# A transformer layer on one core: the order of stages drawn again from a planner with other costs

## The reference

```python
x = x + 0.5 * ffn(layernorm(x))
x = x + attention(layernorm(x))
x = x + 0.5 * ffn(layernorm(x))
```

## Time and profile before

| | us |
|---|---|
| median of 3 executions | 1149.53 |
| lowest and highest of them | 1144.08, 1149.84 |
| profiled execution, its own time | 1146.77 |
| its span, first to last instruction | 1145.5 |
| PE busy | 1014.8 |
| DVE busy | 728.5 |
| ACT busy | 642.0 |
| POOL busy | 486.2 |
| mean granted TensorE clock | 0.963 |

### The profile page before, as it was taken

The page is one execution under the profiler, slowest core; times in us unless marked ns, Lnnn a source line. Parts: engine busy times, 40 slices in busy tenths (PEclk is TensorE's granted clock), DMA queues, the critical chain, the costliest instruction groups (busy, mean ns, idle before and its releaser), DMA issues. The chain is left out here.

```text
span 1145.5 us, 11321 instructions
## 1 busy us (share of the span) xinstructions
PE 1014.8 (89%) x3424; PEld 559.0 (49%) x3424; DVE 728.5 (64%) x1210; ACT 642.0 (56%) x1100; POOL 486.2 (42%) x449
## 2 busy tenths in 40 slices
PE   5989999779899898899999799978997999999992
PEld 3456544446345554344554445444554544446671
DVE  2310119879799988979998999899999721200000
ACT  4334334775674776655687666339778733224441
POOL 3444540556414334335334324714654412245642
PEclk9989999899999899999999899989999999999997
DMA  9966563793834776825587953347885735226666
GB/s 317 328 184 132 97 166 82 192 275 62 207 101 92 172 205 164 223 66 141 126 218 163 228 156 84 94 124 177 177 212 134 167 46 96 70 92 112 129 100 111
DMA packets 69201, 172.53 MB, mean 151 GB/s; under 512 B 12579, under 2 KB 12579, under 8 KB 67015
## 3 DMA queue, kind: packets, MB, share of 16 engines
q0 software_dynamic: 32576, 72.44, 34.8%
q1 hardware_dynamic: 35270, 89.74, 25.0%
q10 hardware_dynamic: 1296, 9.63, 2.4%
HBM read 112.86 MB, written 68.33 MB: 158 GB/s over the span
## 5 line engine op out<-in xcount | busy, mean ns | idle before, releaser
L932 PE MATMUL yps<-w_all,hidden_sb 128*128 x424 | 212.5, 626 | 15.7 <-ACT hidden_sb L1098 15.5
L916 PE MATMUL hps<-w_all,hidden_sb 128*128 x848 | 206.9, 389 | 11.0 <-ACT hidden_sb L1081 10.7
L1720 POOL DMA_INDIRECT xs<-x_normal,rows_i x106 | 121.8, 1149 | 198.9 <-PE xps L907 141.6
L916 PEld LDWEIGHTS hps<-w_all,hidden_sb 128*128 128x128 f32 x848 | 159.7, 195 | 49.4 <-issue 31.1
L1744 POOL DMA_INDIRECT x_rows<-ys,rows_i x56 | 105.2, 1878 | 147.6 <-ACT ys L1111 137.9
L1520 DVE TENSOR_TENSOR_SCAN run<-pwx,trig 128x512 f32<-128x512 f32 x128 | 149.4, 1209 | 20.8 <-ACT trig L1186 20.4
L1111 ACT ACTIVATE ys<-yps,slots 128x512 f32<-128x512 f32 x106 | 72.6, 686 | 110.8 <-PE yps L932 80.4
L932 PEld LDWEIGHTS yps<-w_all,hidden_sb 128*128 128x128 f32 x424 | 80.8, 200 | 87.9 <-issue 85.5
L874 PE MATMUL yps<-sw_sb,hidden_sb 128*128 128x512 f32 x256 | 120.1, 613 | 0.0
L862 PE MATMUL hps<-xnT,sw_sb 128*128 128x512 f32 x256 | 117.8, 612 | 2.1 <-issue 2.1
L1706 POOL DMA_INDIRECT slots<-told,dest_i x64 | 78.1, 1220 | 51.0 <-DVE cmp_a L1389 32.2
(11 more groups left out here) (201 smaller groups left out, 1541.8 us busy)
## 6 DMA issues: line engine op xcount, KB each, us to landing
qx<-q_cols SPq DMA_DIRECT2D x64, 512.0 KB
w_all<-in_w_experts SPq DMA_DIRECT2D x8, 1024.0 KB
x_normal<-xin SPq DMA_DIRECT2D x32, 256.0 KB
xin<-x_rows SPq DMA_DIRECT2D x32, 256.0 KB, 7.1
turns_sb<-in_w_out ACTq DMA_DIRECT2D x3, 1536.0 KB, 7.9
xin<-in_x SPq DMA_DIRECT2D x16, 256.0 KB, 6.0
sum_rows<-ys SPq DMA_DIRECT2D x16, 256.0 KB
xin<-sum_rows POOLq DMA_DIRECT2D x16, 256.0 KB, 5.9
```

The source lines that it names most:

```text
L916: t = PE.matmul(hps[:, bank, 0:H], xT[:, j % 2, c, :], w_all[:, bass.ds(expert[j] + c * H, H)], start=c == 0, stop=c == KC - 1)
L932: t = PE.matmul(yps[:, bank, :], hb[:, j % 2, ec, :], w_all[:, bass.ds(expert[j] + (KC * H + ec * D), D)], start=ec == 0, stop=ec == EC - 1)
L1720: GE.indirect_dma_start(xs[:, j % NX, :], None, xn_rows[PAIR_OF[g]], bass.IndirectOffsetOnAxis(rows_i[:, g % 2, j:j + 1], 0)).then_inc(*xs ...
```

## The change

Costs, crossings and offsets of the planner are replaced. Stages, their instructions, waits and buffers are the same; only the lists of ORDERS differ, and with them the counts at which semaphores are awaited. A cost was the length of a stage; now it is the time from one stage of the engine to the next, and HOP, charged for every step from a stage to a follower, is 0.2 instead of 0.1. The core of the diff (the rest of the costs are lowered in the same manner, by 0.08 to 1.1 us):

```diff
-                piece("PE", s, 3.6, *kept_rows, *start[:1], *blocks_end, bank=[("hps", ("ACT", s))])
-                piece("ACT", s, 0.7, ("PE", s), *([("PE", ("acc", q - 1, TB - 1))] if q else []), table="gelu")
+                piece("PE", s, 3.45, *kept_rows, *start[:1], *blocks_end, bank=[("hps", ("ACT", s))])
+                piece("ACT", s, 0.58, ("PE", s), *([("PE", ("acc", q - 1, TB - 1))] if q else []), table="gelu")
...
-                piece("PE", s, 0.6 if j % AT_ONCE else 1.3, ("POOL", ("bring", g, j), 3.8),
+                piece("PE", s, 0.45 if j % AT_ONCE else 0.95, ("POOL", ("bring", g, j), 3.8),
...
-                piece("PE", s, 1.86, ("ACT", ("x", g, j)),
+                piece("PE", s, 1.74, ("ACT", ("x", g, j)),
...
-                piece("PE", s, 0.4, ("ACT", ("one", g, j)))
-                piece("ACT", s, 0.8, ("PE", s), *([("PE", ("two", g, j - 2))] if j >= 2 else []), table="gelu")
+                piece("PE", s, 0.23, ("ACT", ("one", g, j)))
+                piece("ACT", s, 0.52, ("PE", s), *([("PE", ("two", g, j - 2))] if j >= 2 else []), table="gelu")
...
-                piece("PE", s, 1.86, ("ACT", ("mid", g, j)), bank=[("yps", ("ACT", s))])
-                piece("ACT", s, 0.7, ("PE", s),
+                piece("PE", s, 1.73, ("ACT", ("mid", g, j)), bank=[("yps", ("ACT", s))])
+                piece("ACT", s, 0.59, ("PE", s),
...
-            piece("ACT", ("c_turn", b, n), 2.0, ("DVE", ("c_turn", b, n)), table="sin")
+            piece("ACT", ("c_turn", b, n), 1.81, ("DVE", ("c_turn", b, n)), table="sin")
...
-                    piece("PE", s, 1.9, ("SP", ("c_out", b, half), 2.4), ("SP", ("w_bd",), 12.0), *rows_before_it,
+                    piece("PE", s, 1.73, ("SP", ("c_out", b, half), 3.8), ("SP", ("w_bd",), 12.0), *rows_before_it,
...
-        PARTS = {"job": {2: 652, 3: -380, 4: -82, 6: -504},
-                 "blocks": {1: -389, 3: 798},
+        PARTS = {"job": {2: -357, 4: -260, 6: -1496},
+                 "blocks": {0: 1007, 1: 101, 4: 10},
                  "head": {},
-                 "tail": {0: -319, 1: 1414, 2: -298, 3: 283},
-                 "steps": {2: 407}}
+                 "tail": {1: 27},
+                 "steps": {1: -1517}}
-        KINDS = {("ACT", "mid"): -175,
-                 ("ACT", "norm"): 880,
-                 ("ACT", "o_rows"): 556,
-                 ("ACT", "one"): -59,
-                 ("ACT", "x"): -132,
...
-                 ("PE", "gT"): -2768,
-                 ("PE", "hidden"): -415,
...
+        KINDS = {("ACT", "a_q"): -279,
+                 ("ACT", "a_spread"): -58,
+                 ("ACT", "mid"): -725,
+                 ("ACT", "one"): -188,
+                 ("ACT", "two"): -1518,
+                 ("ACT", "x"): -67,
...
+                 ("DVE", "c_times"): -1129,
+                 ("DVE", "c_turn"): -88,
...
+                 ("PE", "hidden"): -1850,
+                 ("PE", "mid"): 3087,
...
         URGENT = {
-            ("ACT", "c_turn"): {0: -804, 1: 297},
-            ("ACT", "two"): {2: -35, 4: -95},
-            ("DVE", "c_turn"): {0: -25, 1: 1196, 2: -92, 3: -968},
...
+            ("ACT", "c_turn"): {2: -89},
+            ("ACT", "mid"): {1: -1518},
+            ("DVE", "c_turn"): {3: 312},
...
-        HOP = 0.1
+        HOP = 0.2
```

More of the change, by code:

```diff
@@ L335, in plan_job @@
-            piece("ACT", ("chunks", q), 0.6, ("PE", ("chunks", q)), *([("PE", ("logits", q - 1))] if q else []))
-            piece("PE", ("logits", q), 0.9, ("ACT", ("chunks", q)), *start[2:], bank=[("xps", ("DVE", ("rank", q)))])
-            piece("DVE", ("rank", q), 1.7, ("PE", ("logits", q)), *start[2:], *([("DVE", ("gates", q - 1))] if q else []),
+            piece("PE", ("chunks", q), 1.0, *kept_rows, *start[:1], bank=[("xps", ("ACT", ("chunks", q)))])
+            piece("ACT", ("chunks", q), 0.48, ("PE", ("chunks", q)), *([("PE", ("logits", q - 1))] if q else []))
@@ L338, in plan_job @@
+            piece("PE", ("logits", q), 0.8, ("ACT", ("chunks", q)), *start[2:], bank=[("xps", ("DVE", ("rank", q)))])
+            piece("DVE", ("rank", q), 1.5, ("PE", ("logits", q)), *start[2:], *([("DVE", ("gates", q - 1))] if q else []),
                   *([("DVE", ("place", g - 1))] if g and not second else []))
-            piece("ACT", ("gates", q), 0.3, ("DVE", ("rank", q)), *([("DVE", ("gates", q - 1))] if q else []), table="exp")
-            piece("DVE", ("gates", q), 1.7, ("ACT", ("gates", q)), *([("PE", ("gT", q - 1))] if q else []),
+            piece("ACT", ("gates", q), 0.15, ("DVE", ("rank", q)), *([("DVE", ("gates", q - 1))] if q else []), table="exp")
@@ L341, in plan_job @@
+            piece("DVE", ("gates", q), 1.5, ("ACT", ("gates", q)), *([("PE", ("gT", q - 1))] if q else []),
                   *([("POOL", ("scatter", g - 2, GTS[g - 2] // 2 - 1), 2.0)] if g > 1 else []))
-            piece("PE", ("gT", q), 0.7, ("DVE", ("gates", q)), bank=[("xps", ("DVE", ("gT", q)))])
-            piece("DVE", ("gT", q), 0.7, ("PE", ("gT", q)), *([("PE", ("acc", q - 1, TB - 1))] if q else []))
+            piece("PE", ("gT", q), 0.45, ("DVE", ("gates", q)), bank=[("xps", ("DVE", ("gT", q)))])
@@ L344, in plan_job @@
+            piece("DVE", ("gT", q), 0.6, ("PE", ("gT", q)), *([("PE", ("acc", q - 1, TB - 1))] if q else []))
             blocks_end = [("PE", ("two", g - 1, NBS[g - 1] - 1))] if g and not second else []
@@ L402, in plan_blocks @@
                     last = [("SP", ("w_rows", JOBS[q][1]), 12.0) for q in GROUPS[g]] if JOBS[z][0] == 1 else []
[L403 removed]
+                piece("POOL", ("add", g, j), 1.65, ("ACT", s), *last)
             if JOBS[z][0] == 2:
@@ L431, in plan_head @@
                 free += [("DVE", ("a_den", b - 1))] if i == HALVES and b else []
-                piece("PE", s, 3.7, *kept_rows, weights, *free, *before, bank=[("misc", ("DVE", s))])
+                piece("PE", s, 3.45, *kept_rows, weights, *free, *before, bank=[("misc", ("DVE", s))])
                 piece("DVE", s, 3.0, ("PE", s))
@@ L436, in plan_head @@
                   *([("PE", ("c_out", b - 2, HALVES - 1)), ("PE", ("a_spread", b - 2, HALVES - 1))] if b >= 2 else []))
-            piece("ACT", ("a_p", b), 0.7, ("DVE", ("a_p", b)), table="exp")
+            piece("ACT", ("a_p", b), 0.55, ("DVE", ("a_p", b)), table="exp")
             piece("DVE", ("a_fall", b), 4.0, ("ACT", ("a_p", b)))
@@ new lines, in macaron @@
+                 "steps": {1: -1517}}
[5 more added lines that the diff above has]
+                 ("ACT", "x"): -67,
+                 ("DVE", "a_mem"): 103,
+                 ("DVE", "c_scan"): -46,
+                 ("DVE", "c_times"): -1129,
+                 ("DVE", "c_turn"): -88,
+                 ("DVE", "place"): 82,
+                 ("PE", "a_mem"): 226,
+                 ("PE", "a_q"): -35,
+                 ("PE", "a_spread"): 654,
+                 ("PE", "c_out"): 4,
+                 ("PE", "hidden"): -1850,
+                 ("PE", "mid"): 3087,
+                 ("PE", "o_gate"): -5,
+                 ("PE", "one"): 48,
+                 ("PE", "two"): -421,
+                 ("PE", "x"): -186,
+                 ("POOL", "add"): -233}
```

111 lines of the change are left out of this document (50 added, 61 removed).

## The result

The changed kernel takes 1163.24 us (median of 4, 1161.74 to 1168.28), the kernel before beside it on the same chip 1148.43 us (4, 1144.08 to 1149.84). The ratio is 1.0143, 95% interval 1.011 to 1.0176: slower by 14.8 us, where I had forecast 14 us faster. The profiled execution took 1163.97 us with a span of 1162.7 us, against 1145.5 before; the 17.2 us between the spans are what the traces have to explain.

What follows compares the result with a forecast made beforehand. TensorE was taken to wait on the order of ScalarE's queue, not its load; 21.0 us of idle, 28.6 us with clock, was halved to 14.3 us, giving 1135 us from 1149.53, range 1124 to 1147 us.

Steps and rivals of the forecast that it cites:

- Waits that I named: TensorE's waits, mostly in the middle (200 to 910 us): four terms, 6.5 + 7.9 + 4.0 + 2.6 = 21.0 us of idle gone.
- The gate products' wait for the output rows: TensorE's wait for the DMA of the attention's output rows: three fifths of 11.0 us go, 6.5 us.
- The waits before the second product: TensorE's 13 waits for ScalarE in the block chain: doubled HOP takes 0.2 us off each, 2.6 us.
- the 4.00 us at 439.17: TensorE's wait while ScalarE stood before a second-batch wave: goes because those waves get offset -1517, 4.0 us.
- ys scaling at the foot of ACT's queue: Scalings get offset -1518, so next-block copies go in front; two long TensorE waits behind them go, 7.9 us.
- The clock term: In the middle, 28 us of slow clock beside 77.9 us of idle: idle gone saves 0.36 us more per us.
- No term for table switches: ScalarE's function table switch costs the load alone, about 1.3 us, without the skill page's drain; the sum has no term.
- That sum leaves everything else where it is ... I keep half, 14.3 us.: Whole run: new offsets lay other waits bare, so half of the 28.6 us gain is kept, 14.3 us.
- Nothing from the two ends: Start and end of the run: no gain; the last 23 blocks run at 4.11 us each with TensorE nearly full.
- The wave rival: Second batch: waves come late for VectorE's scans, VectorE ends 15 us later, 1160 us; chance 0.09.
- The yps-bank rival: Middle blocks: late ys scalings hold the two yps banks, the second product waits for a scaling, 1164 us; chance 0.12.
- My sign for it (well over 20 us): VectorE's scans, which waited 20.4 us for ScalarE's waves, would wait well over 20 us.

Runs made afterwards that it cites:

- before_pe_minus: Kernel before, with only one of four partial products in the hidden products of the fifth job, 10.3 us less TensorE work: 1150.93 us.
- before_dve_plus: Kernel before, with the scans of steps 6 to 11 of the third batch made twice, 13.4 us more VectorE work: 1159.89 us.
- gelu_offset_out: Changed kernel without two offsets on ScalarE's middle gelus (-725, and -1518 in batch 1): 1162.62 us.
- waves_up: Changed kernel with 15 waves moved two or three places ahead in ScalarE's list: 1168.31 us.
- steps1_zero: Changed kernel without the offset of -1517 on the steps of the second batch: 1158.32 us.
- offsets_only: Kernel before with its costs, crossings and HOP kept and the new offsets put in: 1162.5 us.
- one splice: Every engine's order is that of the kernel before up to step 6 of the second batch, then the changed kernel's: 1169.68 us.

## Why the prediction was wrong

**Waits that I named.** The gate products' wait for the output rows fell from 11.0 us to 1.4 over the whole run, more than the 6.5 us taken. The waits before the second product fell by 9.6 us, against 2.6. Before the second transpose 21.0 became 6.8, and the 4.00 us at 439.17 went with their kind (8.5 us before, 1.9 after). Sized low, right in sign: in the middle these four kinds together lost 39 us, where I had taken 21.0. What came in their place took most of it back: 18.0 us for late gelus and 9.0 for the gathers' DMA were not in the list before. That the idle time fell by 10.8 us in the end, close to half of my 21.0, is luck and no proof of the half. No run says which line of the diff did it; an offset of 3087 on PE's second transposes, for which I had no term, is a candidate.

**ys scaling at the foot of ACT's queue.** Wrong. The hold of ACT before a scaling did not go (22.2 us in 6 waits for the additions' DMAs in the middle before, 18.4 in 6 after); near the same place as before it is longer, and the gelu behind it now holds a bank (after, ACT and then PE; the earlier trace rows had 5.45 us):

```profile
259.16 0.69 ACT L1117 ACTIVATE ys<-yps,slots 128x512 f32<-128x512 f32 x1 [8.03 <-DMA x_rows<-ys,rows_i]
```

```profile
260.99 3.48 PE L922 MATMUL hps<-w_all,hidden_sb 128*128 x8 [6.01 <-ACT hidden_sb L1104]
```

An offset chooses only among the stages that are ready on paper, so the foot of the queue on paper did not keep this scaling from standing in front of others on the chip.

**The clock term, 0.36 us per us of idle.** Wrong. The middle's idle time fell by 10.8 us and its clock went from 0.96 to 0.95; the last stretch, now with bare waits, fell from 0.97 to 0.92. PE's busy time rose by 7.6 us for the same instructions. In `before_pe_minus` it is 1009.2 us, 5.6 less than before, where 10.3 us of instructions went, and in `before_dve_plus`, which changes nothing on PE, it is 8.1 us more.

**No term for table switches.** Right, and the row behind it holds after the change too:

```profile
232.62 1.28 ACT L1104 ACT_TABLE_LOAD   x1
233.92 0.62 ACT L1104 ACTIVATE hidden_sb<-hps,bias_of 128x128 f32<-128x128 f32 x2
```

ACT has 1104 instructions instead of 1100, four table loads more (129 instead of 125), and is busy 3.8 us longer. The further 1380 ns of drain that the Trainium skill's page "ScalarE: Activation LUTs", section "What ACT_TABLE_LOAD costs", states do not show in these rows either: the next activation starts 1.30 us after the load does.

**"That sum leaves everything else where it is ... I keep half, 14.3 us."** This is the step that failed. It takes PE's idle time in the middle as the currency, and it is none: 10.8 us less of it went with 17.2 us more of span, because 17.5 us more came behind 910 us and PE's busy time rose by 7.6, and 10.3 us of PE work less in `before_pe_minus` gave nothing. The runs showed two other quantities in its place: the start of the last scan, 28.3 us later, and what is left to stand behind it, a stretch 11.1 us shorter. I had written that DVE "sets when the last attention rows and so the last blocks can begin", and priced it only inside that half.

**"Nothing from the two ends."** Wrong. The last 23 blocks do run as before (156.5 and 157.8 us from `place` to the end), but the stretch from the last scan to `place` is 12.4 us shorter, bought with a later scan, and the first scan is 4.5 us late. An order that runs filler early has it no more when the tail waits.

**The rivals.** The wave rival, given 0.09 and 1160 us, is nearest to what happened: 15.6 us more of waits for waves and 1163.2 us. Its place was too narrow: they stand in batches two to four (22 us more), of which removing the offset on the second batch's steps gives back 5 us of time. My sign for it (well over 20 us) is there, 36.0. The yps-bank rival's own sign is not: the second product waited 0.8 us for scalings in the whole run. A like mechanism came on the hps banks (18.0 us); `gelu_offset_out` took only 4.2 us of it away, so what the rest costs was not measured.

**What stays open.** Why the pair of before is better than the ten other orders with offsets that were run (1155.8 to 1171.8 us) is told here as which waits it has, not why its draw has them. Nor is it shown that the waits for waves are the cause of the late scans in after: the one run that aimed at them alone, `waves_up`, made fewer of them and later scans. `steps1_zero` points to one more order that wasn't tried: the same with the four `acc` stages behind the output rows' products. With the 25.5 us of before in place of 40.2 it would end up to 14.7 us earlier; the 16 us of `acc` would have to fit into the 46 us in which PE idles behind its last scan.

## What to carry to other kernels

Where two engines and the queue between them are nearly full, price a reordering by the milestone that the tail hangs on (here the last scan) and by what is left to fill the tail, not by the idle time of the fullest engine: here 14 us added to TensorE or VectorE cost about 12, and 10 us taken from the fuller one gave nothing. Look also at what the queue between them waits for: ScalarE stood 46.2 us at the head of the waves before and 16.8 after. But take it as a place to look and not as a measure, since `offsets_only` with 41.3 us was as slow as after. Offsets tuned on a planner may belong to its costs: on other costs the old ones kept 5 us of their 39, while the new ones did no worse on the old costs. When both are replaced at once, run the two halves too.

## What the runs showed of the hardware

The same program varies more than I had thought: the kernel before ran from 1137.8 to 1156.0 us beside the experiments, and one splice from 1158.1 to 1178.7 us, the profiled execution being its fastest (span 1156.5). A span of one execution is thus good for where time goes, not for a ratio. TensorE's granted clock did not follow the idle time of a stretch: 67.1 us of idle at 0.95 in the middle after, 77.9 us at 0.96 before.
